# A graph-attention layer on one core: node scores, sorting and last sums shared out anew among the engines

## What is computed

```
h = relu(layernorm(x))
edge_m = concat(h[src], edge_attr) @ a.T          # a is 128 x 256
edge_e = exp(-leaky_relu(edge_m @ a_2[0], 0.2))   # one number for each edge
out = x + segment_sum(edge_e * edge_m, src) / segment_sum(edge_e, src)
```

## Time and profile before

| | us |
|---|---|
| median of three runs | 1207.09 |
| the profiled execution | 1210.7 |
| its span, first to last instruction | 1208.9 |
| TensorE matmul / VectorE / ScalarE / POOL busy | 626.6 / 857.9 / 585.9 / 768.1 |

### The profile page before, as it was taken

One profiled execution on the slowest core, in us unless ns is written; L12 is line 12 of the kernel. 1 busy time (PEld: TensorE's weight loads), 2 busy tenths in 40 slices (PEclk: granted clock), 3 DMA queues, 4 the chain that ended last, 5 costly groups with the idle time before them and its releaser, 6 DMA issues. The chain is left out here.

```text
span 1208.9 us, 22334 instructions
## 1 busy us (share of the span) xinstructions
PE 626.6 (52%) x5452; PEld 528.9 (44%) x5453; DVE 857.9 (71%) x2932; ACT 585.9 (48%) x2008; POOL 768.1 (64%) x814
## 2 busy tenths in 40 slices
PE   1671018223767028211546077771275488889887
PEld 0561015223656016211535056661264477678766
DVE  5856798876858988843546999873465768834677
ACT  1664020445666040542555034982465309978656
POOL 2006737577777777777777777777777777777000
PEclk9785558556877558555677578985587559979998
DMA  9939959589895652757879385974977529399583
GB/s 299 330 135 351 369 185 331 199 251 393 262 334 160 218 165 87 247 177 267 300 247 305 103 289 185 369 255 160 363 235 232 171 82 282 124 312 289 214 269 108
DMA packets 188561, 291.76 MB, mean 241 GB/s; under 512 B 19288, under 2 KB 125879, under 8 KB 188215
## 3 DMA queue, kind: packets, MB, share of 16 engines
q1 hardware_dynamic: 143940, 162.33, 41.3%
q10 hardware_dynamic: 19442, 75.36, 18.5%
q0 software_dynamic: 25088, 53.04, 12.3%
HBM read 159.04 MB, written 131.61 MB: 240 GB/s over the span
## 5 line engine op out<-in xcount | busy, mean ns | idle before, releaser
L507 POOL DMA_INDIRECT ordered_rows<-feed,dest x784 | 761.5, 971 | 352.7 <-issue 246.2
L755 PE MATMUL psum<-back,hots 128*128 128x129 f32 x2128 | 329.3, 312 | 36.2 <-DVE hots L1056 27.1
L755 PEld LDWEIGHTS psum<-back,hots 128*128 128x128 f32 x2128 | 293.8, 218 | 76.5 <-issue 74.1
L631 ACT ACTIVATE apart<-lanes,back 128x128 bf16<-128x128 bf16 x532 | 169.4, 389 | 236.1 <-PE psum L755 197.6
L725 PE MATMUL psum<-score_parts,place_hot 128*128 128x50 bf16 x2352 | 101.1, 206 | 276.3 <-DVE place_hot L976 257.0
L588 ACT ACTIVATE feed<-feed 128x128 f32<-128x128 f32 (+1 forms) x784 | 238.7, 387 | 0.0
L725 PEld LDWEIGHTS psum<-score_parts,place_hot 128*128 128x128 bf16 x2352 | 92.5, 111 | 286.2 <-DVE place_hot L976 265.1
L976 DVE TENSOR_SCALAR place_hot<-place_rows,lane 128x1024 bf16<-128x1024 bf16 (+1 forms) x98 | 50.1, 511 | 188.6 <-SPq L378 179.0
L580 ACT ACTIVATE feed<-leaky 128x8 f32<-128x8 f32 (+1 forms) x98 | 20.4, 208 | 325.6 <-DVE leaky L1008 325.6
L985 DVE SCALAR_TENSOR_TENSOR junk<-feed,psum 128x128 bf16<-128x128 f32 x784 | 169.9, 280 | 0.0
L1039 DVE TENSOR_TENSOR acc<-acc,psum 128x387 f32 (+1 forms) x133 | 73.5, 553 | 58.8 <-PE psum L755 47.5
(11 more groups left out here) (145 smaller groups left out, 490.3 us busy)
## 6 DMA issues: line engine op xcount, KB each, us to landing
ordered_rows<-empty SPq DMA_DIRECT2D x19, 3696.0 KB, 19.6
back<-ordered_rows ACTq DMA_DIRECT2D x133, 528.0 KB
feed<-in_edge_attr SPq DMA_DIRECT2D x97, 512.0 KB
place_rows<-places SPq DMA_DIRECT2D x98, 256.0 KB, 4.9
ordered_rows<-feed,dest POOLq DMA_INDIRECT x784
self_part<-acc ACTq DMA_DIRECT2D x1, 3234.0 KB, 11.5
feed<-self_part SPq DMA_DIRECT2D x1, 3234.0 KB
out<-feed SPq DMA_DIRECT2D x6, 448.0 KB
```

The source lines that it names most:

```text
L507: pool.indirect_dma_start(out=ordered, out_offset=bass.IndirectOffsetOnAxis(ap=dest[:, n:n + 1], axis=0), in_=feed[:, n * ROW:(n + 1) * RO ...
L631: act.activation(apart[:, v * P:(v + 1) * P], lanes[:, :], ACT.Abs, bias=tags[:, u, PLACE:PLACE + 1], scale=-1.0).then_inc(apart_done, 1)
L755: last = pe.matmul(psum[:, bass.ds(outs[u], FEAT + 1)], hots[:, hot_buffer(k) * GT + u, :], back[:, n:n + FEAT + 1], start=False, stop=u = ...
```

## The change

1. *Node scores.* ScalarE takes all 49 ReLUs in place, POOL multiplies seven windows at a time by a weight row, ScalarE sums each window's 128 terms with an accumulating copy. The products for the node rows, three windows at a time, move into a stage of their own, ("self",), after the eighth group, with the store of `self_part`; rstd is applied at the end.
2. *Order.* VectorE counts chunk 0 before the statistics; group 0 is started ahead of rank 0; the tables are entries of their own. Eight groups instead of six go ahead of count 1, three instead of four between count 1 and rank 1. SP stores and loads the places after the first load and the first fill, then issues the rest; constants are written early.
3. *Sorting.* The hots are 50 compares with a number each. In chunks 1 to 4 VectorE multiplies the counts of the upper 25 buckets by their hots, TensorE adds these with 25 bf16 products, and the picks are split: VectorE 25 in three buffers, ScalarE 25 (`hot * shift`) in two.
4. *Chunk 4.* All three banks are added at once; ScalarE clears the two others from the third step on; VectorE makes six of eight one-hots.
5. *End.* TensorE transposes the sums unscaled, three windows at a time; the inverse is applied with the result; every second unit's self part is scaled by ScalarE and added by POOL. The last two scatters, of empty tiles, are left out.

The core of the diff:

```diff
+DVE_HALF, DVE_BUFS, ACT_BUFS = 25, 3, 2
+NW = 3
...
+LAST_TILES = COLS + 1 - (GROUPS - 1) * GT
...
-    ("stats",), ("count", 0), ("rank", 0), ("nodes",), ("feed", 0, 1), ("feed", 1, 1), ("feed", 2, 4), ("count", 1), ("feed", 6, 4), ("rank", 1),
-    ("feed", 10, 11),
-    ("pairs", 0, 0, 3, 21, 4), ("count", 2), ("feed", 33, 5), ("rank", 2), ("feed", 38, 13),
...
+    ("count", 0), ("stats",), ("rank", 0), ("nodes",), ("feed", 0, 2), ("table", 0), ("feed", 2, 6), ("self",), ("count", 1), ("feed", 8, 3),
+    ("rank", 1), ("table", 1), ("feed", 11, 10),
+    ("pairs", 0, 0, 3, 21, 4), ("count", 2), ("feed", 33, 5), ("rank", 2), ("table", 2), ("feed", 38, 13),
...
+    ("pairs", 2, 0, 2, 79, 4), ("count", 4), ("feed", 87, 1), ("rank", 4), ("table", 4), ("pairs", 2, 2, 5, 88, 3), ("feed", 97, 1),
...
+            load(0, 0, 0)
             sp.wait_ge(placeT_copied, BLOCKS)
             for b in range(BLOCKS):
                 n = min(P, TILES - b * P)
                 sp.dma_start(places[b * P:b * P + n, :], placeT[0:n, b * P:(b + 1) * P]).then_inc(place_stored, 16)
+            sp.wait_ge(pool_set, 4)
+            fill(0, 0)
             sp.wait_ge(place_stored, 16 * BLOCKS)
             for k in range(AHEAD):
                 load_places(k, k)
+            load(1, 1, 1)
+            for r in range(1, CHUNKS[0] + 1):
+                fill(r, 0)
+            for k in range(2, RG):
+                load(k, k, k)
...
+            pool.wait_ge(weights_copied, 4)
+            for i in range(WINDOWS // RG):
+                at = slice(RG * i, RG * i + RG)
+                pool.wait_ge(relu_done, RG * (i + 1))
+                pool.tensor_tensor(node_terms[:, at, :], acc_w[:, at, 0:FEAT],
+                                   node_w[:, :].rearrange("p (a f) -> p a f", a=1).to_broadcast([P, RG, FEAT]),
+                                   ALU.mult).then_inc(terms_done, 1)
...
+                    for u in range(LAST_TILES if isinstance(r, int) and r == ROUNDS - 1 and k == RG - 1 else GT):
...
+                at = slice(NW * n, NW * n + NW)
+                pool.wait_ge(self_scaled, n // 2 * NW + NW)
+                pool.tensor_tensor(fin_x[:, at, 0:FEAT], fin_x[:, at, 0:FEAT], fin_self[:, at, 0:FEAT], ALU.add).then_inc(pool_added, 1)
...
+            def node_relu():
...
+                for w in range(WINDOWS):
+                    act.activation(acc[:, w * ROW:w * ROW + FEAT], acc[:, w * ROW:w * ROW + FEAT], ACT.Relu,
+                                   bias=moments[:, w, 0:1]).then_inc(relu_done, 1)
+                for w in range(WINDOWS):
+                    act.wait_ge(terms_done, w // RG + 1)
+                    act.activation(node_terms[:, w, :], node_terms[:, w, :], ACT.Copy, accum_out=score[:, w:w + 1]).then_inc(dots_done, 1)
...
+            def self_rows():
+                def save(n):
+                    at = windows_of(n)
+                    act.wait_ge(self_done, n + 1)
+                    act.copy(acc_w[:, at, 0:FEAT], bank(2 + n % 2, 0, (at.stop - at.start) * P).rearrange("p (k f) -> p k f", f=P))\
+                       .then_inc(self_copied, 1)
+                act.wait_ge(dots_done, WINDOWS)
+                for n in range(FIN_UNITS):
+                    at = windows_of(n)
+                    act.wait_ge(selfT_done, n + 1)
+                    if n >= 2:
+                        act.wait_ge(self_done, n - 1)
+                    act.copy(last_T[:, n % 2, 0:at.stop - at.start, :].rearrange("p k f -> p (k f)"),
+                             bank(n % 2, 0, (at.stop - at.start) * P)).then_inc(selfT_copied, 1)
+                    if n > 0:
+                        save(n - 1)
+                save(FIN_UNITS - 1)
+                act.wait_ge(self_copied, FIN_UNITS)
                 act.dma_start(self_part, acc[:, 0:WINDOWS * ROW]).then_inc(self_saved, 16)
...
+            def shift_chunk(c):
+                tiles = CHUNKS[c] * RT
+                act.wait_ge(hots_done, (c + 1) * BUCKETS)
+                act.wait_ge(bases_done, c + 1)
+                for j in range(DVE_HALF):
+                    b, k, n = DVE_HALF + j, DVE_BUFS + j % ACT_BUFS, (c - 1) * DVE_HALF + j
+                    if j >= ACT_BUFS:
+                        act.wait_ge(shifts_added, n - ACT_BUFS + 1)
+                    act.activation(picked[:, k * tiles:(k + 1) * tiles], hot[:, b * tiles:(b + 1) * tiles], ACT.Copy,
+                                   scale=shift[:, b:b + 1]).then_inc(shifts_done, 1)
...
+                if c == LAST and LAST_STEP + ADD_LAG <= S:
+                    act.wait_ge(acc_done, S - ADD_LAG + 1)
+                    act.copy(psum_sets[:, S % 2, 1:, 0:PER_BANK * (FEAT + 1)],
+                             empty[:, 0, 0:2 * PER_BANK * (FEAT + 1)].rearrange("p (b f) -> p b f", b=2)).then_inc(rest_cleared, 1)
...
                 tiles = CHUNKS[c] * RT
-                first = isinstance(i, int) and i == 0
-                for k in range(BB):
-                    pe.wait_ge(picks_done, c * BUCKETS + i * BB + k + 1)
+                for b in range(DVE_HALF):
+                    k, a = b % DVE_BUFS, DVE_BUFS + b % ACT_BUFS
+                    pe.wait_ge(picks_done, picks_before(c) + b + 1)
                     pe.matmul(ranks(c, SUMS, tiles), ident[:, :], picked[:, k * tiles:(k + 1) * tiles],
-                              start=first and k == 0, stop=k == BB - 1, skip_group_check=True)\
-                      .then_inc(picks_added, 1)
+                              start=False, stop=False, skip_group_check=True).then_inc(picks_added, 1)
+                    pe.wait_ge(shifts_done, (c - 1) * DVE_HALF + b + 1)
+                    pe.matmul(ranks(c, SUMS, tiles), ident[:, :], picked[:, a * tiles:(a + 1) * tiles],
+                              start=False, stop=b == DVE_HALF - 1, skip_group_check=True).then_inc(shifts_added, 1)
+            def count_sums(c):
+                tiles = CHUNKS[c] * RT
+                pe.wait_ge(counted_done, c)
+                pe.wait_ge(picks_done, picks_before(c) + 1)
+                for b in range(DVE_HALF, BUCKETS):
+                    pe.matmul(ranks(c, SUMS, tiles), ident_bf[:, :], count[:, b * tiles:(b + 1) * tiles],
+                              start=b == DVE_HALF, stop=False, skip_group_check=True)
...
+            def self_products():
+                def product(n):
+                    pe.wait_ge(selfT_copied, n + 1)
+                    if n >= 2:
+                        pe.wait_ge(self_copied, n - 1)
+                    for k in range(min(WINDOWS, NW * n + NW) - NW * n):
+                        last = pe.matmul(bank(2 + n % 2, k * P, P), last_T[:, n % 2, k, :], A1w[:, :], start=True, stop=True)
+                    last.then_inc(self_done, 1)
+                pe.wait_ge(relu_done, WINDOWS)
+                for n in range(FIN_UNITS):
+                    if n >= 2:
+                        pe.wait_ge(selfT_copied, n - 1)
+                    for k, w in enumerate(range(NW * n, min(WINDOWS, NW * n + NW))):
+                        last = pe.transpose(bank(n % 2, k * P, P), acc_w[:, w, 0:FEAT], ident[:, :])
+                    last.then_inc(selfT_done, 1)
+                    if n > 0:
+                        product(n - 1)
+                product(FIN_UNITS - 1)
...
-                    if u == DVE_HOTS:
+                        if c == LAST and S >= LAST_STEP + ADD_LAG:
+                            pe.wait_ge(rest_cleared, S - ADD_LAG - LAST_STEP + 1)
...
+                    for w in range(NW * n + NW, NW * n + 2 * NW):
+                        act.activation(fin_self[:, w, 0:FEAT], fin_self[:, w, 0:FEAT], ACT.Copy,
+                                       scale=kept[:, w:w + 1]).then_inc(self_scaled, 1)
...
+                none = bank(CONSTS, ZERO, 1).to_broadcast([P, flat]) if c > 0 else hot[:, 0:flat]
+                for b in range(BUCKETS):
+                    dve.tensor_scalar(hot[:, b * tiles:(b + 1) * tiles], bucket[:, t0:t0 + tiles], float(b), None,
+                                      ALU.is_equal).then_inc(hots_done, 1)
...
+                if c > 0:
+                    dve.wait_ge(ends_done, c + 1)
+                    half = slice(DVE_HALF * tiles, flat)
+                    dve.tensor_tensor(count[:, half], count[:, half], hot[:, half], ALU.mult).then_inc(counted_done, 1)
...
+                count_of, bufs = (BUCKETS, BB) if c == 0 else (DVE_HALF, DVE_BUFS)
...
+                dve.sem_inc(ranked, 1)
+            def table_chunk(c):
...
-                dve.wait_ge(consts_done, 4)
-                start_group(0)
-                dve.wait_ge(self_copied, WINDOWS)
-                full, rest = acc_w[:, 0:WINDOWS, FEAT], score_rest[:, 0:WINDOWS]
+                dve.wait_ge(dots_done, WINDOWS)
+                full, rest = score[:, :], score_rest[:, 0:WINDOWS]
+                done(dve.tensor_tensor(full, full, rstd[:, :], ALU.mult))
...
+                if others is None:
+                    wait()
```

(24 more changed lines are left out.)

286 lines of the change are left out of this document (130 added, 156 removed).

## The result

The changed kernel takes **1189.68 us** (median of 4 runs, 1186.81 to 1191.82) against 1207.53 us for the kernel before beside it: a ratio of 0.9855, 95% interval 0.9825 to 0.9885. It is faster by 17.9 us; 25.7 were forecast, and the time lies in the range of 1168 to 1196. The profiled execution took 1189.83 us with a span of 1188.0, so 20.9 us of span have gone.

A forecast was written before the change was run, and what follows sets the result against it. POOL's 784 indirect DMAs at 1.265 us, 992 us, were taken as a floor under the middle; -26 + 3.7 - 2.4 - 1 = -25.7 us off the 1207.09 us median gave 1181.5 us, range 1168 to 1196.

The forecast's parts named there:

- last sort: Chunk 4's count and rank, behind scatter 79: compares and multiply +2.5 us, count sums +1.2, together +3.7 us slower.
- The start: Up to POOL's first scatter: group 0's landing near 55.5 us is late next; first scatter at 86 us, 9.6 us earlier.
- The two pauses: POOL's pauses at groups 8 and 11: the first goes, 12.5 us of the second stays; shift at group 11 -24 us.
- some 36 us: From first scatter to count 1: SP's landing of group 8 takes 36 us, so count 1 starts at 122 us.
- From there POOL is continuous in both: POOL's scatters from group 11 to 79: no pauses and fewer slow scatters while picks run, -2 us.
- The split picks: Rank 1's picks: bound moves from VectorE to TensorE and little is saved, 24 against 24.4 us.
- Chunk 4: Last chunk's steps: 2.4 to 2.5 us instead of 2.97, -5.5 us at their end, only -2.4 us through the output's inputs.
- Rival A: Early groups stay bound by queues: count 1 at 138, both pauses stay, shift -10, 1196 us; chance 0.15.
- D: Rival: VectorE and ScalarE pick pairs not overlapped; over 1.25 us a pair eats the gain, 1.5 gives about 1214 us; chance 0.04.
- E: Rival: the change does not do what it says, picks and node work hidden both ways, 1207 us; chance 0.03.
- C: Rival: no early start, first scatter at 95, only the first pause saved, 1192 us; chance 0.1.
- B: Rival: warm, early start with first scatter at 81, shorter rank 1 and final stage, 1169 us; chance 0.15.

The follow-up runs named there:

- experiment 7: Changed kernel with group 0 handed on before SP issues the loads of groups 2 to 6: 1179.85 us, ratio 0.9761.
- experiment 10: Changed kernel with the old grouping, six groups ahead of count 1 and four between it and rank 1: 1187.29 us, ratio 0.9829.
- experiment 3: Changed kernel with VectorE waiting for its own result after every fifth compare and its multiply cut into five with waits: 1187.25 us, ratio 0.9840.
- experiment 5: Changed kernel with all picks on VectorE, a wait behind every fifth, no multiply of counts or count sums: 1182.46 us, ratio 0.9799.
- experiment 6: Kernel before without VectorE's wait for its own result behind every pick of ranks 1 to 4: 1210.30 us, ratio 1.0019.
- Experiment 8: Changed kernel with the output's inputs issued at the fourth last step's read-back instead of the last: 1181.66 us, ratio 0.9780.
- experiment 4: Changed kernel with all picks on VectorE without pauses, no multiply of counts or count sums: 1188.81 us, ratio 0.9839.

## Why the prediction was right, and where its sizes were off

The forecast was 1181.5 us, the time 1189.68: right in sign and range, 8.2 us too fast. Of these 4.8 lie in the profiled spans (20.9 gained for 25.7); 3.0 are the gap between the spans and the medians (17.9), since the profiled execution of the kernel before (1210.7 us) lay 3 us above the median and that of the change did not; 0.4 is the later median of the kernel before. In spans, step by step:

| step | forecast | measured |
|---|---|---|
| first scatter | 86 (81 to 95) | 87.45 |
| count 1 starts | 122 | 127.69 |
| pause at group 8; at group 11 | none; 12.5 | none; 8.9 |
| shift at group 11 | -24 | -21.9 |
| from group 11 to 79 | -2 | +4.7 |
| last sort (hots to the first operation behind the picks) | +3.7 | +2.5 |
| from there to chunk 4's first one-hots | 0 | -1.0 |
| output's inputs, against those | -2.4 | -3.3 |
| results | -1 | -2.1 |
| sum, with 0.1 between | -25.7 | -21.0 |

- **The start** held term by term. The landing came at 58.5 for 55.5, 50 picks took 13.97 for 14.7, the sums 0.29 us each. That the landing, not the node work, would be late next was right, and experiment 7 shows it: with it moved, 10 us more go. The seven POOL products (14.3 us) lay in the wait for the landing, as costed at nothing; in experiment 7 that cover is gone and they cost 7 us of small operations.
- **The two pauses.** The first goes, as forecast, but the eight groups ahead of count 1, to which I put it down, are the smaller part: with six (experiment 10) some 2 us of the 16.4 would be left. The larger part is the earlier start and a count 1 that comes sooner. The term "some 36 us" was mis-sized: group 8 was handed on at 125.1, 37.7 us behind the first scatter, and VectorE then prepared it for 2.5 us before count 1, which the term leaves out. The second pause is 8.9 us for 12.5 only because POOL was through with group 10 at 205.3 instead of 199.5, held up by the two long scatters of count 1. What the forecast needed of it, the shift at group 11, was -21.9 for -24: count 1 began 5.7 us late, and 3.5 of these came back by then, since from count 1 to group 11 there were 86.5 us for 90 (the 50 compares, 6.58 us, and the multiply, 3.08, came at the low ends of 6 to 9.5 and 3 to 6, the picks at 22.5 for 24). That these two errors cancel in part is luck.
- **The term that was mis-sized is the -2 us behind "From there POOL is continuous in both"**: +4.7 where -2 stood, 6.7 us lost where the whole shortfall of the spans is 4.8. POOL was continuous, with no pause behind group 11, but its scatters were not as short as costed. The scatters of 5.48, 3.30 and 1.96 us are 7.9 us more than 0.96 each; the fewer slow ones give back some 2.6 (13 in rank 2 at 0.2). I had costed the 50 compares and the multiply by VectorE's time alone, and read POOL's slowing by the port as 0.2 us a scatter, since the earlier trace rows show 1.16. That size belongs to a VectorE that pauses after each pick, which the kernel before takes care to do. Experiments 3, 5 and 6 show that it is the pause that counts.
- **The split picks.** That the bound moves to TensorE was right (two passes every 0.378 us, TensorE 21.9 us busy of 22.6 in rank 1). That the split saves little was too kind: with the pauses thinned out, VectorE alone is as fast without the multiply (21.6 against 22.5 us in rank 1, experiment 5). 24.43 us was the cost of the pauses, not of the picks.
- **The last sort** cost 2.5 us instead of 3.7. VectorE's picks took 20.46 for 20.17 us, and behind the last one it waited longer for TensorE, before and after:

```profile
982.77 0.22 DVE L895 CAST picked<-psum 128x56 int32<-128x56 f32 x1 [1.86 <-PE psum L698]
```

```profile
968.27 0.22 DVE L998 CAST picked<-psum 128x56 int32<-128x56 f32 x1 [2.78 <-PE psum L778]
```

Together these are the 1.2 us forecast for the count sums; the compares and the multiply cost 1.3 us where 2.5 stood. **Chunk 4** took 2.4 to 2.5 us a step and gained 5.6 us for a forecast of 5.5, of which the inputs passed on 3.3 for 2.4. Experiment 8 confirms that they were what the end waited for. The 1.0 us between the sort and chunk 4 is not explained.
- **The rivals.** Rival A's 1196 did not come, though its mechanism is there in part (7.32 us of landing). D's pick pairs came every 0.757 us, the 0.76 of the prediction; its 1.25 was never near. E and C fall with the first scatter at 87.45, and so does B, which had it at 81. One kernel's runs spread by up to 12 us (experiment 4: 1184.2 to 1196.6), in which chance scatters are the likely part; that was argued, not shown.

## What to carry to other kernels

Where POOL issues indirect DMAs back to back, cost each new VectorE instruction also by what it does to POOL: a row of short ones from SBUF to SBUF, or with two SBUF inputs, may stop POOL for as long as the row lasts. A wait of VectorE for its own result every five instructions cost 0.1 to 0.2 us here and ended that (experiments 3 and 5); and a wait that looks needless in a tuned kernel is to be explained before it is costed. When an engine waits for a hand-over, look at what the handing engine issues first: moving three lines there brought 10 us, more than half of what the whole change did.
